# Attention expansions of q sent as three transfers, and both halves sent without a wait for rows of maxima

## What is computed

```python
def layer(x):                       # four of them, each with its own weights
    xn = layernorm(x)
    return x + attention(xn) + feed_forward(xn)

def attention(xn):                  # layers 0, 2 and 3
    q, k, v = (split_heads(xn @ W + b) for W, b in projections)
    scores = einsum('bhqd,bhkd->bhqk', q, k) * scale      # + mask or bias
    return softmax(scores) @ v @ Wo + bo
```

## Time and profile before

| | |
|---|---|
| median of three runs | 2870.99 us |
| the profiled execution's own time | 2863.05 us |
| its span (first to last instruction) | 2861.2 us |
| mean granted TensorE clock, share of 2.4 GHz | 0.931 |
| PE busy | 2431.9 us, 85% |
| DVE busy | 1534.3 us, 54% |
| ACT busy | 1340.6 us, 47% |
| POOL busy | 564.8 us, 20% |
| k expansions, q expansions | 48 transfers each of 576 KB |

### The profile page before, as it was taken

How to read it: one execution, slowest core, us unless ns; L and a number is a source line. 1 busy time by engine, 2 the same in 40 slices (tenths; PEclk the granted TensorE clock), 3 DMA queues, 4 the chain that set the end, 5 groups by cost and what they waited for, 6 DMA issues and landing times. The chain is left out here.

```text
span 2861.2 us, 45685 instructions
## 1 busy us (share of the span) xinstructions
PE 2431.9 (85%) x15607; PEld 1470.4 (51%) x15730; DVE 1534.3 (54%) x4364; ACT 1340.6 (47%) x2454; POOL 564.8 (20%) x591
## 2 busy tenths in 40 slices
PE   4688788899994799999996799988886888898887
PEld 2345444588883466666795344444442433444333
DVE  4577667411112366555533566666646776777663
ACT  3355444544443333333134355555551666666665
POOL 1433333000003654553001111111100001111000
PEclk9899999999997799999998699999996999999999
DMA  3222222377773100000264211111102111111011
GB/s 115 75 72 77 77 71 65 105 213 204 207 209 111 29 23 22 23 26 10 80 195 116 71 43 51 51 52 53 57 15 86 46 51 51 51 46 40 33 39 32
DMA packets 132374, 214.08 MB, mean 75 GB/s; under 512 B 22664, under 2 KB 91824, under 8 KB 125232
## 3 DMA queue, kind: packets, MB, share of 16 engines
q1 hardware_dynamic: 119024, 186.88, 22.4%
q0 software_dynamic: 10240, 20.99, 2.6%
q10 hardware_dynamic: 2880, 3.28, 0.4%
HBM read 158.50 MB, written 51.40 MB: 73 GB/s over the span
## 5 line engine op out<-in xcount | busy, mean ns | idle before, releaser
L534 DVE TENSOR_REDUCE arena<-bank 128x1 f32<-128x512 f32 (+4 forms) x1216 | 725.5, 616 | 491.3 <-PE bank L523 258.7
L609 ACT ACTIVATE arena<-bank 128x512 f32<-128x512 f32 x640 | 374.7, 599 | 422.6 <-PE bank L599 349.2
L517 PE MATMUL bank<-arena 125*128 125x512 bf16 (+3 forms) x1536 | 478.5, 348 | 33.5 <-DMA arena<-q_parts 18.4
L587 PE MATMUL bank<-arena 128*128 128x512 bf16 (+3 forms) x1413 | 407.6, 333 | 106.5 <-ACT arena L609 69.7
L609 ACT ACTIVATE arena<-bank,arena 128x512 f32<-128x512 f32 x512 | 337.7, 688 | 213.7 <-PE bank L587 80.9
L587 PEld LDWEIGHTS bank<-arena 128*128 128x128 bf16 x1536 | 139.3, 101 | 413.4 <-ACT arena L609 255.7
L624 PE MATMUL bank<-arena 128*32 128x512 f32 (+3 forms) x3072 | 333.9, 517 | 1.4 <-ACT arena L609 0.8
L938 POOL DMA_INDIRECT back_rows<-sorted_out,back_now x160 | 154.7, 967 | 515.8 <-PE bank L599 231.3
L517 PEld LDWEIGHTS bank<-arena 125*128 125x128 bf16 x1536 | 146.8, 102 | 206.7 <-DVE arena L534 89.0
L1177 ACT ACTIVATE arena<-bank,arena 128x256 f32<-128x256 f32 x320 | 131.9, 471 | 160.0 <-PE bank L1227 160.0
L1022 PE MATMUL bank<-arena 128*128 128x128 f32 x1664 | 202.5, 275 | 0.3 <-ACT arena L1177 0.3
(11 more groups left out here) (250 smaller groups left out, 3558.2 us busy)
## 6 DMA issues: line engine op xcount, KB each, us to landing
arena<-k_parts SPq DMA_DIRECT2D x48, 576.0 KB
arena<-q_parts SPq DMA_DIRECT2D x48, 576.0 KB
arena<-in_L_ffn_w SPq DMA_DIRECT2D x80, 320.0 KB, 3.6
arena<-in_L_ffn_w SPq DMA_DIRECT2D x80, 258.0 KB, 3.1
arena<-sorted_in SPq DMA_DIRECT2D x104, 128.0 KB, 2.5
sorted_out<-arena SPq DMA_DIRECT2D x104, 128.0 KB, 3.5
arena<-in_L_ffn_w SPq DMA_DIRECT2D x24, 512.0 KB, 4.0
k_parts<-arena SPq DMA_DIRECT2D x24, 384.0 KB
```

Of the source, the lines that this page charges most:

```text
L517: ins = pe.matmul(mx[:, k * w:(k + 1) * w], Qx[0:KMAX, h, q * P:(q + 1) * P], Kx[0:KMAX, h, 0:w], start=(k == 0 or not L.causal), stop=not ...
L534: ins = dve.reduce_max(L.mx[:, g % 2, q, heads[0]:heads[-1] + 1], mx[:, 0:w * len(heads) - far].rearrange("p (j k) -> p j k", k=w - far), ...
L587: ins = pe.matmul(st[:, c:c + w], Kx[:, h, kb * P:(kb + 1) * P], Qx[:, h, T - w:T], start=(c == 0), stop=not (L.causal or far), skip_group ...
L609: act.activation(L.probs[:, n % L.PR, 0:w], st[:, 0:w], ACT.Exp, scale=L.scale).then_inc(L.st_free.sem, 1)
```

## The change

q is expanded by three transfers for each half in place of one: each writes one of the three blocks of 24 partitions, from the same 24 rows in DRAM. The semaphore of each half of q counts 48 in place of 16, and PE waits for 48. The waits for rows of maxima ahead of half 1 (layers 0 and 2) and of half 0 (layer 3) are gone, and so is `L.behind_row`. The k expansions are as they were, and so are the bytes moved.

```diff
-            L.behind_row = {0: 2} if biased else {1: 3}
...
-            L.qx = [s(f"q_expanded{i}_", 16, 1) for i in range(HALVES)]
+            L.qx = [s(f"q_expanded{i}_", 16 * NPART, 1) for i in range(HALVES)]
...
-            q_rows = L.qd.rearrange("d i (o h) t -> o (d i) h t", o=1)
+            q_rows = L.qd.rearrange("d i h t -> (d i) h t")
             for half in range(HALVES):
                 heads = slice(half * H // HALVES, (half + 1) * H // HALVES)
-                if not first and half in L.behind_row:
-                    settle(sp)
-                    sp.wait_ge(L.nmrow.sem, L.nmrow.at(whole(b.index - 1), 16 * L.behind_row[half]))
                 sp.dma_start(copy_of(L.Kx, b)[0:KROWS, heads, :], k_rows[:, :, heads, :].rearrange(
                     "r o h t -> r o (h t)").to_broadcast([NPART * HD, NPART, H * T // HALVES])).then_inc(L.kx[half].sem, 16)
-                sp.dma_start(copy_of(L.Qx, b)[0:KROWS, heads, :], q_rows[:, :, heads, :].rearrange(
-                    "o r h t -> o r (h t)").to_broadcast([NPART, NPART * HD, H * T // HALVES])).then_inc(L.qx[half].sem, 16)
+                for j in range(NPART):
+                    sp.dma_start(copy_of(L.Qx, b)[j * NPART * HD:(j + 1) * NPART * HD, heads, :],
+                                 q_rows[:, heads, :]).then_inc(L.qx[half].sem, 16)
...
-                pe.wait_ge(L.qx[half].sem, L.qx[half].at(b, 16))
+                pe.wait_ge(L.qx[half].sem, L.qx[half].at(b, 16 * NPART))
```

## The result

The changed kernel takes 2901.82 us (median of four runs, 2892.34 to 2913.89), the kernel before, measured beside it, 2868.89 us. The ratio is 1.0115, 95% interval 1.0091 to 1.0139: slower by 33 us, where 53 us faster was forecast. The profiled execution takes 2900.6 us, its span is 2898.8 us, the mean granted clock 0.923 (0.931 before), PE busy 2459.0 us (2431.9 before). In the changed kernel's numbering the score matmul is L584, the mask matmul L596, the product for the maxima L514, the exponential L606, the k expansions L488, the q expansions L491 and the rows of maxima L497.

What follows compares the result with a forecast made beforehand. PE's work and idle time bound the kernel, transfers only where PE waits. 15.5 + 14 + 17 + 0 + 10 + 6 = 62.5 us, less 15%, is 53: 2870.99 to 2818 us; 8-in-10 range 2785 to 2848.

Steps and rivals of the forecast that it cites:

- Twelve engines for q: q expansions: with 24 rows outermost, each transfer runs on twelve engines in place of three.
- How long the expansion lasts: Whole q and k expansion, 2.36 MB: 11.2 us at 211 GB/s, or 9.2 us at the engines' own limit.
- rival 4: Slower: q in 1 KB pieces or on few engines, over 20 us, delaying rows in layers 0 and 2; 2905 us, chance 0.07.
- The starts: Starts of layers 0 and 3: half 0 of q ready at 39.9 and 2179.2, 15.5 us gained (13 to 16).
- Rows in layer 3: PE's waits for rows of maxima in layer 3 fall from 18.8 to 0 to 11 us; 14 us gained.
- How a row is held up: A row of maxima waits for the expansion work left ahead of it, 1.0 to 3.1 us in layer 3.
- rival 1: Rows of maxima keep their delay, perhaps from a fixed queue depth, and the clock gives nothing; 2843 or 2849 us, chance 0.09.
- Rows in layer 2: Earlier half 1 frees row g=3, 17 us gained; row g=2 counts 0, between a loss of 6 and gain of 2.8.
- Layer 0: Rows there do not stall PE, row g=2 comes at the expansions' very end; 6 us gained (0 to 9) from PE's stops.
- Clock: Fewer PE stalls in layers 2 and 3 keep the granted clock higher; 10 us gained (0 to 22).
- Dropping the wait: Removing waits for rows ahead of q halves buys 0 by itself; it moves half 1 off row g=3 and POOL's scatters.
- The stops of PE in layer 0: PE, ACT and POOL stop twice per batch during POOL's scatters; less half 1 traffic there gives 6 us (0 to 9).

Runs made afterwards that it cites:

- spread kernels: Kernel before, q in three transfers to every third partition, k's parts stored as (d, j); ratio 0.9934 with old waits, 0.9918 all behind third row, 0.9792 mixed waits.
- padded rows: Changed kernel with DRAM rows of q and k 18 KB apart instead of 16, k stored by three transfers; 2889.68 us on the first chip, ratio 1.0068 on the third.

## Why the prediction was wrong

**Twelve engines for q: right.** There is no tail at 0.20 and the share is 0.69 to 0.72.

**How long the expansion lasts: the step that failed.** I set 9.2 to 11.2 us, from the rate of k's transfers (211 GB/s) and of a large load (341 GB/s). Neither writes 24 adjacent partitions from many engines at once. It was 14.2 to 18.6 us, 15.7 on average, or 151 GB/s. Rows 3 held a warning: the rate per engine fell from 25 GB/s with three to 17 with twelve, and I took the 17 as the floor. The prediction's own threshold, "below about 200 already eats the gain of layer 3", was passed by far. Yet the rate stayed above the 115 GB/s from which rival 4 was to decide, so the loss came at a higher rate than that rival allowed.

**The starts.** 15.5 us were to come. Half 0 of layer 0 was ready at 44.1 and not 39.9:

```profile
32.64 0.81 SPq L488 DMA_DIRECT2D arena<-k_parts  x1
44.10 0.58 PE L514 MATMUL bank<-arena 125*128 125x128 bf16 x4 [6.45 <-DMA arena<-q_parts]
```

That is 11.5 us behind k's issue in place of 15.4, where I had 7.6. The waits for q fell by 18.4 - 10.3 = 8.1 us. The same cause, for the most part: the pieces of this expansion took 0.64 us on average and not the 0.43 I took from before. With 0.64 the prediction's own sum, 12 x 0.64 + 2.4, gives 10.1 us; the 1.4 us that are left no run explains.

**Rows in layer 3.** 14 us were to be gained; 43.0 - 18.8 = 24.2 were lost. The row at 2330.29 finds 10.7 us of block ahead of it (to 2341), and lands with its end; so it is in all seven batches, where PE goes on within 1 us of the block's end.

**How a row is held up: a second step that was wrong.** The prediction let a row wait for the work that is left ahead of it ("finds 1.0 to 3.1 us of work"). But in the trace of before the row of 2317.31 has landed by 2323.76, and the tail goes on behind it at a share of 0.20, to 2333.2. After, in layer 2, the row of 1709.66 has landed by 1718.90, and the block still moves 95 GB/s:

```profile
1718.90:1722.10 3.20, 3.20 (x9) 1.05 (x10) 0.65 (x2) 1.33 (x4) 1.10 (x1) 0.66 0.42 95
```

A row with next to nothing beside it took 2.6 us (issued at 2200.54, landed by 2203.14 in the trace of before). The first of the two rows above took 6.4 us, 3.8 more, with pieces of 0.31 us; the second took 9.2 us, 6.6 more, with pieces of 0.55 us. Both are the time of 12 pieces on one engine. That is my estimate, and what sets the number stays open. It is the ground that rival 1 gave, "a fixed depth of queue and not the backlog": a row waits for a dozen pieces at most, or for the end of the block if that comes sooner. Rival 1 kept the row's delay as it was; in fact the pieces became twice as long, and the delay grew with them. The row of 164.90, which the prediction called undisturbed, had q's tail beside it as well (share 0.18 from 165 to 166); it was quick because less than 2 us of the tail were left.

**Rows in layer 2.** That moving half 1 frees the row of g=3 was right: the ten waits of rows 1 became six, all at g=2. But each is longer, up to 5.7 us, 22.8 us in all, where I had g=2 between a loss of 6 and a gain of 2.8 and a net gain of 17.

**Layer 0.** I wrote that the row of g=2 "comes at the very end of the expansions". It comes in their middle: 23.1 us. This is the place that rival 4 named, and it had 20 us for it. That its 2905 is close to the 2901.8 measured is luck all the same: it had 14 us more of waits in layer 2, where there were 2.8, nothing in layer 3, where there were 24.2, nothing for the clock, and left out what the starts give back. Its ground was other too (few engines or 1 KB pieces, over 20 us); the real one, a full set of engines at half speed, I had not among the rivals.

**Clock.** It was to give 10 us back. It went the other way, 0.931 to 0.923, and in layer 2 it makes 11.9 of the 17.6 us of four batches. I counted the clock behind the stalls that go, and none behind stalls that might come.

**Dropping the wait "buys nothing by itself": right as an average** (ratio 0.9994), and misleading. The wait kept half of the block out of the way of the row of g=2 in layers 0 and 2. Cheap to lose while the tail was on three engines, it was worth 1% once q was on twelve (1.0016 with it, 1.0115 without).

## What to carry to other kernels

Before a bulk transfer is spread over more engines, reckon its time from a row with the same destination partitions, and look at which small, urgent transfer is issued while it runs: here that one waited for some dozen pieces of the big one, and each piece had become twice as long. If such a block is slow, first look for the gap between two urgent transfers that it fits into, and tie its start to the landing of the one ahead; that alone took the changed kernel from 1.0115 to 0.994 on the second chip and to 0.985, with the better place for each layer, on the third. If the partitions can be chosen, try partitions far apart for one transfer, and rows in DRAM that are not 16 KB apart.

## What the runs showed of the hardware

Eleven to twelve engines busy gave 132 and 159 GB/s in two windows, 151 on average, into 24 adjacent partitions, and 187 GB/s into every third one, with the same source and bytes. In the spread kernels q has eight rows outermost and the share is lower, 0.59 at 164 GB/s: fewer engines, each a little faster (17 GB/s for 16).

The stops of PE in layer 0 beside POOL's scatters, of which the prediction hoped to recover a part, don't come from the expansions alone. The kernel with every third partition ran on the first and on the third chip. PE's waits in layer 0 (45:545), first chip:

```profile
PE bank L584 <- ACT arena L606: 40.1, 14, 14.6
```

On the third chip the list for the same stretch begins with

```profile
PE bank L406 <- DVE xn L382: 15.6, 7, 2.8
```

and the wait of L584 for ACT is not in its first seven; the span is 2777.1 us for 2846.1. The kernel before is faster there too, 2808.56 us for 2872.18 and 2870.34. What makes PE stop on the one chip and not on the other stays open, as does whether it always does. The ratios may owe something to the missing stops as well: a stall that a stop used to cover can show, or the other way round. Two kernels ran on both chips. Every third partition gave 2847.95 for 2872.18 us (0.992) on the first and 0.9935 on the third, padded rows 2889.68 for 2872.18 us (1.006) and 1.0068, so for these two the difference is small.
